# Last phase of a fused GNN and expert-FFN kernel: the scaled relu written by ScalarE, the rows of x added to it by the gather, and a pipeline two steps longer

## The reference, cut to what matters

```
h = layernorm(x)
for l in range(3):
    rst = relu(h @ W_self[l] + segment_mean(h[src], dst) @ W_neigh[l] + b[l])
    h = rst / max(sqrt(sum(rst * rst)), 1e-12)
x = x + h                                  # the kernel's x2
xn = layernorm(x) ; xn = layernorm(xn) * g + b
sel = top-2 experts of softmax(xn @ Wg), their outputs weighted
x = x + layernorm(xn + sel) * out_g + out_b
```

## Time and profile before

| what | value |
|---|---|
| time, median of 3 runs | 2375.69 us (2375.51 to 2376.06) |
| the profiled execution's own time | 2379.8 us |
| its span in the profile | 2378.1 us |
| PE busy over the span | 2115.0 us (89%) |
| DVE busy | 1870.2 us (79%) |
| POOL busy | 1311.5 us (55%) |
| ACT busy | 994.2 us (42%) |

### The profile page before, as it was taken

One profiled execution on the slowest core, in us unless ns is written; L12 is line 12 of the kernel. 1 busy time (PEld: TensorE's weight loads), 2 busy tenths in 40 slices (PEclk: granted clock), 3 DMA queues, 4 the chain that ended last, 5 costly groups with the idle time before them and its releaser, 6 DMA issues.

```text
span 2378.1 us, 45348 instructions
## 1 busy us (share of the span) xinstructions
PE 2115.0 (89%) x15947; PEld 1163.1 (49%) x15947; DVE 1870.2 (79%) x4201; ACT 994.2 (42%) x1698; POOL 1311.5 (55%) x1475
## 2 busy tenths in 40 slices
PE   2998899888799999997999999995599999999998
PEld 0443344334344444443444444442466666666676
DVE  4778887556688878875778888874699999999985
ACT  1322111111333333332333333333776777777662
POOL 3760004770555555553344444435688888888864
PEclk9999999999899999998999999997699999999999
DMA  4553335783455555554444445444333333333311
GB/s 126 143 148 120 107 123 126 112 112 105 135 171 164 168 164 169 167 168 132 150 168 164 168 164 173 164 163 142 115 121 121 125 117 125 125 121 125 125 50 44
DMA packets 146471, 323.01 MB, mean 136 GB/s; under 512 B 30793, under 2 KB 30967, under 8 KB 146247
## 3 DMA queue, kind: packets, MB, share of 16 engines
q1 hardware_dynamic: 90487, 154.68, 22.5%
q0 software_dynamic: 55760, 165.43, 21.4%
HBM read 175.81 MB, written 144.83 MB: 135 GB/s over the span
## 4 chain that ended last, share of the span: by engine, by line
PE 44%; DVE 25%; issue 13%; POOL 11%; ACT 6%; DMA 1%; DVEq 0%; POOLq 0%; ACTq 0%
PE psS L486 16%; PE psY L486 12%; PE psY L1696 8%; POOL slot_table L628 4%; DVE R L1321 4%; DVE YB L1205 3%; POOL node_info L628 3%; DVE HT L1198 3%; ACT HH L875 2%; POOL scl L723 2%; PE psT L1613 2%; DVE HH L1345 2%; DVE w_n L1465 1%; DVE area L1365 1%; PE psA L1653 1%
## 5 line engine op out<-in xcount | busy, mean ns | idle before, releaser
L486 PE MATMUL psY<-w_n,HT 128*128 128x512 f16 x2844 | 673.9, 388 | 83.5 <-DVE HT L1198 78.9
L486 PE MATMUL psS<-w_s,HT 128*128 128x512 f16 x2844 | 652.5, 379 | 0.0
L486 PEld LDWEIGHTS psY<-w_n,HT 128*128 128x128 f16 x2844 | 266.5, 99 | 477.7 <-DVE HT L1198 173.4
L486 PEld LDWEIGHTS psS<-w_s,HT 128*128 128x128 f16 x2844 | 268.6, 98 | 280.2
L867 ACT ACTIVATE RR<-R 128x512 f32<-128x512 f32 x237 | 149.4, 630 | 310.9 <-DVE R L1321 307.9
L730 POOL DMA_INDIRECT y_rows<-YB,poutT x158 | 160.8, 1018 | 189.7 <-DVE YB L1205 161.2
L723 POOL TENSOR_TENSOR scl<-ssm,halfpow 128x1 f32<-128x1 f32 x158 | 88.6, 561 | 286.9 <-DVE ssm L1339 286.9
L486 PE MATMUL psS<-w_w,raw 128*128 128x512 f16 x948 | 217.5, 379 | 0.0
L831 ACT ACTIVATE HH<-R 128x512 f16<-128x512 f32 x79 | 49.7, 629 | 376.2 <-DVE R L1186 343.7
L1345 DVE SCALAR_TENSOR_TENSOR HH<-RR,scl,HH 128x512 f16<-128x512 f32 x158 | 118.8, 752 | 88.8 <-ACT HH L875 88.8
L1215 DVE SCALAR_TENSOR_TENSOR SB<-psS,downs,bias 128x512 f32<-128x512 f32 x237 | 177.9, 751 | 12.4 <-PE psS L486 9.6
(11 more groups left out here) (281 smaller groups left out, 3880.0 us busy)
## 6 DMA issues: line engine op xcount, KB each, us to landing
self_rows<-SB SPq DMA_DIRECT2D x236, 256.0 KB
Sl<-self_rows SPq DMA_DIRECT2D x158, 256.0 KB
X<-in_x_dram SPq DMA_DIRECT2D x78, 256.0 KB
y_rows<-YB SPq DMA_DIRECT2D x78, 256.0 KB
raw<-in_L_gnn_W_neigh_dram SPq DMA_DIRECT2D x12, 256.0 KB
raw<-in_L_gnn_W_self_dram SPq DMA_DIRECT2D x12, 256.0 KB
y_rows<-YB,poutT POOLq DMA_INDIRECT x158, 3.0
raw<-in_L_ffn_W_dram SPq DMA_DIRECT2D x8, 256.0 KB
```

The lines of the kernel that those rows point to most:

```text
L486: mm = eng.matmul(acc, lhs[:, a, c, :], w[:, bpart, c, :], start=(n == 0), stop=(stop and n == 3 * KC - 1))
```

## The change

- DVE's `x2` goes. ACT gets `h3` at offset +3, first in its list: a Copy of RR with the scale scl, written into the X2 ring. POOL's `by_node` goes and `add_x` comes at offset +3, first in POOL's list: the same indirect DMA of 128 rows of x, which now goes straight to the X2 tile and adds to what is there (`compute_op=ALU.add`). It waits for `h3` of its own step.
- `x2_stats` and `x2_mean_var` go from +3 to +1 and wait for that DMA. All stages behind them, on all engines, go two steps later.
- The X2 ring gets 18 tiles; the two new ones are the tiles of `X`, which no longer serve for the rows of x. `xob` waits for `x2_stats` of its own step in place of `x2`.
- `norm3` and `relu` wait for `h3` of the tile before, where they waited for `x2`.

```diff
-X2_RING = 16
+X2_RING = 18
...
-        self.x2 = sem("f3_x2")
+        self.h3 = sem("f3_h3")
+        self.x2 = [sem(f"f3_x2_{i}") for i in range(4)]
...
-        X2 = ring(0, X2_RING)
+        X2 = ring(0, 16) + [X[i][:, :] for i in range(2)]
...
+            def add_x(t):
+
+                t = t.own
+                pool.wait_ge(f3.h3, (t + 1).n)
+                pool.indirect_dma_start(X2[t.slot(X2_RING)], None, x[:, :],
+                                        bass.IndirectOffsetOnAxis(ap=pinT[:, t.t:t.t + 1], axis=0),
+                                        bounds_check=node_limit, oob_is_err=False, compute_op=ALU.add
+                                        ).then_inc(f3.x2[t.slot(4)], 16)
+
...
-                pool.wait_ge(f3.x2, min(t.t + 6, T))
+                pool.wait_ge(f3.bnx, min(t.t + 6, T))
...
-            run_tiles(T, [(7, gather), (-2, xob), (5, by_node), (4, norm3), (3, pow_of_group), (-9, zr_of),
-                          (-10, put_out)], 2)
+            run_tiles(T, [(3, add_x), (7, gather), (-4, xob), (4, norm3), (1, pow_of_group), (-11, zr_of),
+                          (-12, put_out)], 2)
...
+            def h3(t):
+
+                i = t.slot(2)
+                act.wait_ge(ph[3].sc, (t + 1).n)
+                act.wait_ge(ph[3].rr, (t + 1).n)
+                t = t.own
+                after(act, f3.o, (t + (1 - X2_RING)).n)
+                act.activation(X2[t.slot(X2_RING)], RR[i][:, :], ACT.Copy, scale=scl[:, i:i + 1]).then_inc(f3.h3, 1)
+
...
-            run_tiles(T, [(4, lambda t: carry_hi(t, 3)), (-2, txc), (-8, fhi), (4, lambda t: relu(t, 3)),
-                          (4, sum_squares3), (4, carry_rest_in), (-7, weights_in), (-1, xn), (-1, xhi),
-                          (-3, gate_tanh), (-7, gelu)], 2)
+            run_tiles(T, [(3, h3), (4, lambda t: carry_hi(t, 3)), (-4, txc), (-10, fhi), (4, lambda t: relu(t, 3)),
+                          (4, sum_squares3), (4, carry_rest_in), (-9, weights_in), (-3, xn), (-3, xhi),
+                          (-5, gate_tanh), (-9, gelu)], 2)
...
-            def x2(t):
-                i, q = t.slot(2), t.slot(X2_RING)
-                dve.wait_ge(s.sc, (t + 1).n)
-                dve.wait_ge(s.rr, (t + 1).n)
-                t = t.own
-                dve.wait_ge(s.xg[i], t.landed(2))
-                after(dve, f3.o, (t + (1 - X2_RING)).n)
-                dve.scalar_tensor_tensor(X2[q], RR[i][:, :], scl[:, i:i + 1], X[i][:, :], ALU.mult, ALU.add
-                                         ).then_inc(f3.x2, 1)
-
             def x2_stats(t):
                 t = t.own
-                dve.wait_ge(f3.x2, (t + 1).n)
+                dve.wait_ge(f3.x2[t.slot(4)], t.landed(4))
+                after(dve, f3.aggx, t.t)
                 dve.bn_stats(st6[:, :], X2[t.slot(X2_RING)]).then_inc(f3.bnx, 1)
...
-            run_tiles(T, [(-8, hs), (3, x2), (2, group_scales), (-4, confidences), (3, x2_stats),
-                          (4, lambda t: combine(t, 3)), (-3, logits), (-8, flo), (-3, largest), (3, x2_mean_var),
-                          (-3, largest_index), (6, lambda t: one_hot(t, 3)), (-3, gaps), (3, group_vars),
-                          (-9, z_stats), (-3, hots), (-9, z_mean_var), (-10, result), (-9, z_gain), (-1, xlo)], 2)
+            run_tiles(T, [(-10, hs), (0, group_scales), (-6, confidences), (1, x2_stats),
+                          (4, lambda t: combine(t, 3)), (-5, logits), (-10, flo), (-5, largest), (1, x2_mean_var),
+                          (-5, largest_index), (6, lambda t: one_hot(t, 3)), (-5, gaps), (1, group_vars),
+                          (-11, z_stats), (-5, hots), (-11, z_mean_var), (-12, result), (-11, z_gain), (-3, xlo)], 2)
...
-            run_tiles(T, [(4, lambda t: aggregate(t, 3)), (-2, turn_x), (-9, down), (4, carry_rest), (-7, turn_w),
-                          (-7, up), (-7, spread_w), (-2, gate)], 2)
+            run_tiles(T, [(4, lambda t: aggregate(t, 3)), (-4, turn_x), (-11, down), (4, carry_rest), (-9, turn_w),
+                          (-9, up), (-9, spread_w), (-4, gate)], 2)
```

More of the change, by code:

```diff
@@ L703, in gather, with by_node @@
                                             bounds_check=node_limit, oob_is_err=False).then_inc(s.g[i], 16)
-                def by_node(t, s=s, l=l):
+                def by_node(t, s=s):
                     i = t.slot(2)
[L708 to L714, removed]
+                    after(pool, s.r, (t + -1).n)
+                    pool.indirect_dma_start(Sl[i][:, :], None, Sd0[:, :],
                                             bass.IndirectOffsetOnAxis(ap=pinT[:, t.t:t.t + 1], axis=0),
-                                            bounds_check=node_limit, oob_is_err=False
-                                            ).then_inc((s.x if l == 1 else s.xg)[i], 16)
+                                            bounds_check=node_limit, oob_is_err=False).then_inc(s.x[i], 16)
                 def norm(t, s=s, l=l):
@@ L756, in norm3 @@
                 pool.wait_ge(s.dv2, (t + 1).n)
-                after(pool, f3.x2, (o + -1).n)
+                after(pool, f3.h3, (o + -1).n)
                 pool.tensor_scalar(ssm[:, i:i + 1], ss[:, i:i + 1], 1e-24, None, ALU.max).then_inc(f3.ssf, 1)
@@ L865, in relu @@
                 else:
-                    after(act, f3.x2, (t.own + -1).n)
+                    after(act, f3.h3, (t.own + -1).n)
                 act.activation(RR[i][:, :], R[i][:, :], ACT.Relu).then_inc(s.rr, 1)
```

## The result

| | before | changed |
|---|---|---|
| median of the runs | 2376.06 us (2375.51 to 2382.04, 5 runs) | 2390.07 us (2388.40 to 2396.19, 5 runs) |
| ratio, 95% interval | 1 | 1.0054 [1.0034, 1.0073] |

2340 us was predicted, with 2326 to 2395 as the range: the time lies in the range, but it moved the other way. The profiled execution of the changed kernel took 2396.19 us, 6 us above its median. Of the difference of its span to the one before, 16.4 us, 4.9 arise ahead of the phase that was changed: the first `aggregate` starts at 1640.58 us in place of 1635.72.

What follows compares the result with a forecast made beforehand. DVE was taken as the bound, at 8.655 us a step. Before, 67 x 8.655 = 579.9; after, 65 x 8.0 + 23.9 = 543.9; the difference, -36.0 us, off the median 2375.69 gave 2340 us, range 2326 to 2395.

Steps and rivals of the forecast that it cites:

- the price of `add_x`: On POOL: issuing the accumulating DMA costs what `by_node`'s plain one costs, 1.22 us; twice that was the upper bound.
- the new step: Middle of phase 3: a step of 8.0 us, between PE's floor 7.83 and POOL's need 8.11, lowered by fewer DVE two-operand instructions.
- What bounds the kernel before: Phase 3: DVE, busy 33.89 of 34.62 us a group, 5.05 of it lost through `xob`; PE's floor 7.83 a step.
- `x2` off DVE, `h3` on ACT: DVE's own work falls 0.75 to 6.46 us a step; ACT rises to 6.87, covered by `relu`'s wait for `combine`.
- one of the signs that the prediction had named for being wrong: On ACT: `h3` waiting for scl would show the forecast wrong.
- `xob` behind `x2_stats` frees the CAST: `xob` on POOL can no longer begin before DVE's CAST is done; the CAST returns to 0.17 us from 1.95.
- Rival 3: The accumulating DMA makes POOL the bound: 0.45 us extra issue breaks even, 1.22 extra gives 2426 us; chance 0.24.
- Then `xob` meets `one_hot` or `result`, where DVE has about 1 us to spare: POOL's two DMAs take `xob` past `flo`, to DVE instructions with about 1 us of slack.
- The depth: Two more steps of filling at 4.76 us and of draining at 7.19: 23.9 us, against two fewer full steps.
- rival 2: DVE stays hampered: `xob` catches `flo` or `result`, POOL waits in `norm3`; step 8.2 to 8.5, 2366 us at 8.4; chance 0.20.
- The landing of the sums: `x2_stats` on DVE needs the accumulated rows only two steps later, some 14 us after `add_x`'s issue.
- Seven times as dear: The accumulating DMA would have to be seven times as dear to be felt by `x2_stats`.

Runs made afterwards that it cites:

- a_plain: The changed kernel with the DMA of `add_x` as a plain gather, without accumulation (scaled relu missing from the output): 2378.24 us, 0.9984 of the kernel before.
- a_memset_long: The changed kernel with POOL's `xob` replaced by a 128x1216 memset that reads nothing (output bias missing): 2348.19 us, 0.9881 of the kernel before.
- a_noxob: The changed kernel with `xob` left out (output bias missing): 2336.77 us, 0.9803 of the kernel before.
- b_xob_late: The kernel before with `xob` waiting for `x2_stats` of its step in place of `x2`, nothing else: 2357.36 us, 0.9912 of the kernel before.
- b_deep: The kernel before with the two steps of pipeline depth alone, `x2` staying on DVE: 2394.12 us, 1.0045 of the kernel before.
- a_light: The changed kernel with two small POOL instructions, the max of `norm3` and the add of `zr_of`, moved to DVE: 2394.61 us, 1.0051 of the kernel before.
- a_memset_long_plain: The changed kernel with `xob` replaced by a 128x1216 memset and `add_x` a plain gather (bias and scaled relu missing): 2333.51 us, 0.9814 of the kernel before.

## Why the prediction was wrong

Two terms failed: the price of `add_x`, and the meetings in "the new step". The step came out 0.73 us above the forecast's 8.0. Taking the first back is worth 0.19 us a step (a_plain); taking away the meeting of `xob`, with 0.15 us of its length, 0.69 (a_memset_long). The parts in their order:

**What bounds the kernel before**: right. DVE full, a seventh of that through `xob` (5.05 of 33.89 us), PE's floor at 7.83 (a_noxob runs at 7.83 through the whole middle).

**`x2` off DVE, `h3` on ACT**: right. ACT's wait for `combine` fell from 38 to 10 us in 300; `h3` takes 0.72. What holds up ACT anew is scl, 45.4 us in 300, one of the signs that the prediction had named for being wrong.

**`xob` behind `x2_stats` frees the CAST**: right, and in the kernel before worth 0.9% by itself (b_xob_late).

**`add_x` at the price of a plain issue, 1.22 us**: wrong. It took 1.66, +0.44 us a step. The argument from the number of rows held for plain DMAs only. Rival 3 had put the point that decides at 0.45 us over 8.11, and that is about what came: 8.11 + 0.44 = 8.55, a change of nothing. But this term alone does not explain the miss: with `add_x` at 1.24 us (a_plain) the step was 8.54 and not 8.0, and with `add_x` at 1.65 and `xob` gone (a_noxob) it was 7.83.

**"The new step", 8.11 less what DVE's two-operand instructions no longer take from POOL**: wrong, and this is the step that turned nothing into a loss. It was taken for granted that less of DVE means fewer meetings. The changed kernel's are nearly as many as before, 4.66 us of DVE's time in a group against 5.05, and they fall where POOL pays for them. The sum that came is 8.11 + 0.44 (`add_x`) + 0.42 (the max, 0.27 to 0.69) - 0.09 (`put_out`) - 0.15 (zv) - 0.04 (the gathers) = 8.69, where 8.73 was measured. Over 65 steps 8.73 gives 567.5 + 23.9 - 579.9 = +11.5 us, and +14 was measured. The relief that I counted on is there, 0.28 where 8.0 in place of 8.11 took 0.11, and the new meeting of `xob`, `xlo` and `norm3` takes more than it. a_memset_long puts a number on that meeting by experiment: without it, and with a POOL instruction 0.15 us shorter than `xob`, the step is 8.05. "Then `xob` meets `one_hot` or `result`, where DVE has about 1 us to spare" was right in one step of four, where it is `result`; in the other three it is `xlo`, and the sentence forgot that the victim holds POOL back in its turn.

**The depth**, 23.9 us less two steps, +6.6 in all: roughly right, 8.1 us in phase 3 and 10.7 in the runs of b_deep. The filling cost 7.5 us more in the changed kernel (81.7 for 74.2).

That the time lies within the range is no merit of the argument: the range took in rival 3, and the forecast was a gain of 36 us. Rival 3 was the case that came, with half of its price from another source; that `xob` catches `result` and ACT waits for scl is of rival 2. The landing of the sums, 5.2 us after the issue, was never waited for in the middle, as said. "Seven times as dear" has no row behind it: a plain one lands after 4.0 us (a_plain), so 14 us would be three and a half times.

## What to carry to other kernels

When two engines hold each other back, taking work off one of them need not make their meetings fewer: here it shifted the phase between them (the changed kernel, a_plain, a_light, and b_xob_late by one wait). Before such a change, ask which instruction of the other engine stands where the freed time will be, and who waits for the victim; taking the long reading instruction off the shared resource (here `xob`, 1.4% by itself in the kernel before) was worth more than making room around it. A full engine whose busy time holds waiting (0.68 us of work shown as 2.5) is not full of work: subtract it first, and go for its cause. Price a new kind of DMA by doubt, not by the plain one, when its issuing engine has no slack.

## What the runs showed of the hardware

- An indirect DMA of 128 rows that accumulates takes GpSimd 1.65 us to issue (a_memset_long) where the plain one takes 1.04 (a_memset_long_plain). It lands 5.2 us after its issue (4.0 plain), and the software queue's share of the 16 engines' time rises from 29.1% (a_plain) to 39.6% (changed) of 300 us for some 34 of them.
- The holding back goes both ways: VectorE's `xlo`, delayed by `xob`, then delays a GpSimd instruction of 128x1, which shows as 0.69 us in place of 0.30 behind the memset, and of 0.25 behind `xob` itself where VectorE is idle. The Trainium skill, "SBUF — State Buffer", section "Who interferes with whom", says that a VectorE instruction with two SBUF inputs contends with a GpSimd one that reads SBUF and not with one that only writes: the memset agrees, 1.13 us long and `xlo` at 0.68 us. It is not so for `one_hot`, an f16 TENSOR_SCALAR of 128x128: beside a memset and a gather's issue it took 2.00 us in place of 0.30 (a_memset_long_plain).
- The 1216-column memset took 1.13 us and the 512-column one 0.56; `xob`, which reads two operands of 512 columns, 1.28.
